# Reordering the last three blocks' steps on TensorE, ScalarE and VectorE in a fused chain of conditioned residual layers

## The reference, cut to what matters

```
x = x + _L0(x, cond)      # low-rank weight decoded from cond, per entry
x = x + _L1(x, cond)      # modulated linear layer, clipped
x = x + _L2(x, cond)      # adapter down, relu, up
# _L3:
h = _ln(_ln(x, pw_g[id], pw_b[id]), cp_g[id4], cp_b[id4])
t = _ln(x, tm_g[id4], tm_b[id4]);  s = _ln(x, ms_g[mask], ms_b[mask])
cat = concat(w0*h, w1*t, w2*(x+mem), w3*(x+noi), w4*(x+res), w5*s)
x = x + _ln(silu(cat @ W1 + b1) @ W2 + b2, int_g, int_be)
```

## Time and profile before

| | us |
|---|---|
| median of 3 executions | 549.65 |
| lowest, highest | 542.51, 550.52 |
| the profiled execution | 539.84 |
| its span | 538.0 |
| TensorE busy in the span | 495.4 (92%) |
| VectorE busy | 407.3 (76%) |
| GpSimd busy | 390.0 (72%) |
| ScalarE busy | 326.5 (61%) |

### The profile page before, as it was taken

One profiled execution on the slowest core, in us unless ns is written; L12 is line 12 of the kernel. 1 busy time (PEld: TensorE's weight loads), 2 busy tenths in 40 slices (PEclk: granted clock), 3 DMA queues, 4 the chain that ended last, 5 costly groups with the idle time before them and its releaser, 6 DMA issues.

```text
span 538.0 us, 9870 instructions
## 1 busy us (share of the span) xinstructions
PE 495.4 (92%) x3408; PEld 354.2 (66%) x3408; DVE 407.3 (76%) x707; ACT 326.5 (61%) x622; POOL 390.0 (72%) x365
## 2 busy tenths in 40 slices
PE   2967968999999999999999999999999999996893
PEld 2944644767677676767676767676767777675682
DVE  1848876768788787878797978787878878885663
ACT  4583647446666575667576667575757665557522
POOL 7468797789777878696968787778777784874221
PEclk9987977899999999999999999999999999998998
DMA  8897714625352252516170707061625241131102
GB/s 300 237 300 190 193 45 95 154 65 122 97 122 78 73 167 60 179 35 204 25 213 0 232 6 208 31 188 51 169 72 154 87 92 40 36 102 57 39 2 78
DMA packets 35621, 61.83 MB, mean 115 GB/s; under 512 B 5985, under 2 KB 18045, under 8 KB 35212
## 3 DMA queue, kind: packets, MB, share of 16 engines
q1 hardware_dynamic: 29532, 44.16, 29.4%
q0 software_dynamic: 5344, 16.87, 10.6%
q10 hardware_dynamic: 720, 0.48, 0.3%
HBM read 52.63 MB, written 8.87 MB: 114 GB/s over the span
## 4 chain that ended last, share of the span: by engine, by line
PE 76%; DVE 10%; ACT 4%; issue 4%; POOL 3%; DMA 1%; DVEq 0%; POOLq 0%; ACTq 0%
PE ps_c L898 12%; PE ps_c L900 11%; PE ps_c L899 11%; PE ps_d L944 9%; PE ps_a L974 6%; PE ps_d L958 6%; PE ps_a L992 3%; PE ps_b L931 3%; PE ps_b L992 3%; PE ps_a L986 3%; DVE tm_t_l L1426 2%; DMA set_wdec<-in_W_dec 1%; PE ps_b L915 1%; PE ps_b L898 1%; PE ps_c L529 1%
## 5 line engine op out<-in xcount | busy, mean ns | idle before, releaser
L1491 POOL DMA_INDIRECT pw_rows<-in_pw,gidx x64 | 63.0, 984 | 17.9 <-issue 17.1
L944 PE MATMUL ps_d<-xm_t,l_w 128*128 128x512 f32 x128 | 59.2, 605 | 0.3 <-DVE h L1417 0.3
L1200 ACT ACTIVATE h<-h,nb_h,rstd_h 128x256 f32<-128x256 f32 x64 | 33.2, 590 | 33.8 <-POOL nb_h L1515 33.7
L1500 POOL TENSOR_TENSOR xm_t<-x_t,style 128x1024 f32<-128x1024 f32 x16 | 30.5, 1905 | 27.9 <-DVE x_t L1330 27.9
L1530 POOL TENSOR_TENSOR h<-xhat,pw_rows 128x1024 f32<-128x1024 f32 x16 | 38.0, 2372 | 11.2 <-ACT xhat L1200 10.7
L944 PEld LDWEIGHTS ps_d<-xm_t,l_w 128*128 128x128 f32 x128 | 23.5, 192 | 25.0 <-issue 23.1
L1549 POOL TENSOR_TENSOR w_up<-up_rep,ugub 128x1024 f32<-128x1024 f32 x16 | 37.9, 2367 | 2.2 <-issue 2.0
L958 PE MATMUL ps_d<-x_t,down_w 128*64 128x256 f32 x256 | 34.1, 413 | 5.8 <-DVE x_t L1352 5.8
L1535 POOL TENSOR_TENSOR h<-h,pw_rows 128x1024 f32<-128x1024 f32 x16 | 38.2, 2390 | 1.3
L1551 POOL TENSOR_TENSOR w_up<-w_up,ugub 128x1024 f32<-128x1024 f32 x16 | 38.2, 2387 | 1.3
L898 PE MATMUL ps_b<-w_h,act_t_l 128*128 128x256 f32 x128 | 38.4, 300 | 0.4 <-DVE act_t_l L1439 0.4
(11 more groups left out here) (239 smaller groups left out, 1537.2 us busy)
## 6 DMA issues: line engine op xcount, KB each, us to landing
ugub<-ugub_scratch SPq DMA_DIRECT2D x32, 512.0 KB, 6.5
x_t<-in_x_t SPq DMA_DIRECT2D x16, 512.0 KB
out<-y_out SPq DMA_DIRECT2D x15, 512.0 KB, 8.1
set_wdec<-in_W_dec SPq DMA_DIRECT2D x2, 1920.0 KB, 9.5
set_wdec<-in_int_W SPq DMA_DIRECT2D x1, 1536.0 KB, 9.9
set_wdec<-in_nets_rows SPq DMA_DIRECT2D x1, 1152.0 KB, 12.5
pw_rows<-in_pw,gidx POOLq DMA_INDIRECT x64
set_wdec<-in_nets_W SPq DMA_DIRECT2D x1, 768.0 KB, 5.0
```

Of the source, the lines that this page charges most:

```text
L944: m = eng.matmul(ps_l1[:, o, :], l1_w[:, k, o * P:(o + 1) * P], xm_t[:, k, :], start=k == 0, stop=k == KB - 1)
L1200: m = eng.activation(out[:, j, :], src[:, j, :], ACT.Identity, bias=nb[k][:, j:j + 1], scale=rstd[k][:, j:j + 1])
L1491: eng.indirect_dma_start(pw_rows[c.ring][:, j, :], None, t["pw"], bass.IndirectOffsetOnAxis(ap=gidx[c.ring][:, j:j + 1], axis=0)).then_inc ...
```

## The change

Three `end` lists are put into another order; no step is added or taken out, and the lists of GpSimd and of the DMA queue (SyncE) are the same.

```
 TensorE
-  (pe_w1_tm, 14), (pe_xht, 15), (pe_cp, 15), (pe_w1_h, 14), (pe_tm, 15), (pe_shift, 15),
+  (pe_w1_tm, 14), (pe_w1_h, 14), (pe_xht, 15), (pe_cp, 15), (pe_tm, 15), (pe_shift, 15),
 ScalarE
-  (act_hnorm, 14), (act_sil0, 13), (act_hh, 14), (act_sil1, 13), (act_x3, 15),
-  (act_msh, 14), (act_xnorm, 15), (act_tmh, 14), (act_onehot, 15), (act_ysquare, 13),
-  (act_x3h, 15), (act_xht, 15), (act_sil0, 14), (act_hnorm, 15), (act_sil1, 14),
+  (act_hnorm, 14), (act_sil0, 13), (act_sil1, 13), (act_hh, 14), (act_x3, 15),
+  (act_xnorm, 15), (act_msh, 14), (act_tmh, 14), (act_onehot, 15), (act_ysquare, 13),
+  (act_x3h, 15), (act_sil0, 14), (act_sil1, 14), (act_xht, 15), (act_hnorm, 15),
 VectorE
-  (v_tmprod, 15), (v_sil1, 14), (v_hprod, 15), (v_tmlow, 15), (v_msprod, 15),
-  (v_hlow, 15), (v_mslow, 15), (v_ygain, 14), (v_ynorm, 14), (v_sil0, 15),
+  (v_sil1, 14), (v_tmprod, 15), (v_hprod, 15), (v_tmlow, 15), (v_hlow, 15),
+  (v_msprod, 15), (v_mslow, 15), (v_ygain, 14), (v_ynorm, 14), (v_sil0, 15),
```

## The result

| | before | after |
|---|---|---|
| median, us | 547.02 (4 executions) | 536.32 (4 executions) |
| lowest, highest, us | 542.51, 550.52 | 535.06, 536.55 |
| profiled execution, span, us | 539.84, 538.0 | 535.06, 533.2 |

The ratio is 0.9863, 95% interval 0.9831 to 0.9895: 1.4% faster. It compares executions in the faster of the kernel's two states; the two medians by themselves would give 0.980, because two of the four executions of before took about 550 us. The forecast was a saving of 5.7 us, 1.0%, and a median of 543.9.

A forecast was written before the change was run, and what follows sets the result against it. TensorE bounds the kernel, stopping for ScalarE and VectorE steps late in their lists. Losses of 7.6 us less new stops of 0.8 and 1.2 leave 5.6; the walk's 5.7 off 549.65 gives 543.9 us, range 534 to 549.

The forecast's parts named there:

- rival 3: Whole executions: most fall like the lower one, giving median 536.8 or 534.1 us with the same mechanism; chance 0.14.
- Block 13's bank 1: ScalarE's silu pair begins near 481.4 and ends near 482.6, so TensorE's 1.18 us loss goes.
- Block 15's `xhat`: ScalarE's norm runs 486.2 to 488.1, leaving TensorE a stop of 0.8 us where 3.24 were.
- The clock: TensorE's W2 of block 13: 1.43 us lost at 1.2 GHz behind the 3.17 us stop is saved.
- h part ahead of the transposes: TensorE, block 14's h part moved forward: a new 1.2 us stop at block 15's `pe_tm`, waiting for `xh_t`.
- The covers: Block 15 on VectorE: h's product is ready 0.9 us and s's low part 0.8 us before TensorE asks.
- rival 2: Block 15's h product or s's low part comes late, costing about 1 us more: 545.0 us; chance 0.12.
- The sum: W2 of block 14 starts near 511.0 and the end moves 5.7 us earlier: span 532.3, median 543.9.
- The clock row: Profile of the changed kernel: a digit under 9 behind slice 36 would show the prediction wrong.
- the median before: Whole kernel: 549.65 us, 9.8 above the profiled execution, taken as it is as base for the 5.7 us saving.
- Rival 1: TensorE's clock dips behind a remaining stop of 0.8 or 1.2 us; 1.43 us stays, 545.4 us; chance 0.11.
- rival 5: Clock stays low from the 0.8 us stop to block 15's `pe_tm`: 6.0 us slower, 555.7 us; chance 0.03.

The follow-up runs named there:

- Run 6: Kernel before with 20 matmuls of constants put into TensorE's 3.2 us stop ahead of L1006 of block 14; median 539.84 us, ratio 0.9979.
- Run 3: Changed kernel with TensorE's old list: block 15's transposes ahead of block 14's h part again; median 539.11 us, ratio 0.9931 to the kernel before.
- run 5: Changed kernel with VectorE's product of s of block 15 ahead of h's low part again; median 536.97 us, ratio 0.9929 to the kernel before.
- run 2: Changed kernel with ScalarE's list at block 13 put back as before; median 542.75 us, ratio 1.0011 to the kernel before.
- run 4: The whole changed kernel measured again, 12 executions; median 536.75 us, ratio 0.9925 to the kernel before.
- run 1: Kernel before with only ScalarE's list at block 13 reordered: bank 1's silu ahead of h's copy, x's norm ahead of s's copy; median 537.22 us, ratio 0.9897.
- run 7: Changed kernel with block 15's transposes ahead of block 14's h part and xh_t ahead of both silus; median 538.46 us, ratio 0.9889 to the kernel before.

## Why the prediction was right

It was right in direction and mechanism, and in how much the change takes off the tail. The time was not: 536.32 us was measured and 543.9 forecast, a miss of 7.6 us that is larger than the saving itself. What came is rival 3, the spread of executions with the same mechanism, at 536.8 us; it had a chance of 0.14 and is why the range reached down to 534. The mechanism first, step by step, all shifted by the 1.0 us that the traces differ at 484:

- *Block 13's bank 1.* Forecast: silu pair from about 481.4, no wait at L1070. The trace has 482.44 - 1.0 = 481.4, and none.
- *Block 15's `xhat`.* Forecast 486.2, stop 0.8. Measured 487.21 - 1.0 = 486.2, stop 0.74. The copy of s at 489.02, its low part at 490.09 (forecast 489.1 on the old axis): covered as said.
- *The clock.* I took 1.43 us as saved because the 3.17 us stop caused the dip. Run 6, where the stop is filled and the dip is gone, bears that out.
- *h part ahead of the transposes.* Forecast: a new stop of 1.2 us released by `xh_t`. Measured 1.19. Run 3 shows what the move is worth: without it the stop is 2.39.
- *The covers.* h's product of block 15 ends at 505.43 + 1.23 = 506.66 and TensorE asks at 507.62: 0.96 us, forecast 0.9. s's low part ends at 513.21 + 1.23 = 514.44, forecast on this axis 514.4, and TensorE asks at 515.17: 0.73 us, forecast 0.8. Neither broke; rival 2 did not come.
- *The sum.* W2 of block 14 begins at 511.90 - 1.0 = 510.9; forecast 511. Tail shorter by 5.81 us; forecast 5.7. The span, forecast 532.3 from an execution that began as that of before did, came out at 533.2, of which 1.0 lies ahead of the change.
- *The clock row.* A digit under 9 behind slice 36 was to be a sign of being wrong. The row has one, the 7 of slice 40, but the fall lies behind TensorE's last matmul (524.51), so the sign was drawn too widely; that of before has an 8 there too.

The size of the median was off for a reason outside the change. The term that failed is the median before, 549.65 of three executions, which I took as it was. Over 60 further executions of before its medians were 542.41 and 542.05, and none was above 548.25. 542.2 less 5.8 is 536.4. So two of the first three executions were unusually slow, by chance or for a cause that is not known, and the mechanism has no part in that difference.

Two things in the prediction need mending. Rival 1, the dip that stays, was placed against the changed kernel on the ground that 0.45 and 1.17 us had cost no clock; run 5 shows a dip behind a stop of 1.19, with about the same price, 1.5 us. The trace of one execution could not rule it out. That the profile of the first result shows none is in part luck: of four profiles with this stop one has the dip. The Trainium skill, "TensorE: Matmul & The Clock Gate", section "A second HAM failure mode: psum-queue depth-cycling", says that short idles between groups of matmuls can come often enough for the clock to swing between its two rates. The traces bear this out only in part: run 5 has one fall, behind one stop, and no repeated swing, and the two profiles of the changed kernel have none. And the price of the dip behind the 3.17 us stop was taken as one number, 1.43; run 2 shows it at over 2.5. So the whole change may remove more than 5.7 us in some executions and give 1.5 us back in others. How often each happens, and so the average, was not measured: the traces show one execution each, and the sums of whole executions mix it with the start of the kernel.

## What to carry to other kernels

When lists of steps are written out by hand, walk the steps through with durations from the trace: each start is the later of "inputs there" and "engine free". Here that gave tails to within 0.2 us in every experiment in which the clock stayed up. What a walk doesn't give is the clock: every stop of TensorE of 1.19 us or more carries a further 1.4 us or more at risk here, so a step that fills a stop can pay even if it makes nothing else earlier (run 6). And where executions differ by 1%, compare traces from a marked instruction behind the part that varies, not spans.

## What the runs showed of the hardware

The granted clock fell from 1.00 to 0.50 (2.4 to 1.2 GHz) behind stops of 3.17, 3.19, 2.39 and 1.19 us, and not behind stops of 1.17, 1.15 and, in three other profiles (first result, runs 2 and 4), 1.19 us. It fell at the end of the stop at the earliest (run 2) and 1.8 us behind it at the latest (run 5), and stayed down for 3.4 us in three of the four cases (before, where the prediction's rival 5 had read 4, and runs 3 and 5) and for 6.8 in run 2. The price of one fall was 1.4 us at the least and over 2.5 at the most. That the stop is the cause was tested for the one of 3.17 us alone, by filling it (run 6); for the shorter ones it is argued from the order in time. I had expected a stop of one length to have one price.

The start of the kernel takes different times in different executions, though its code is the same: those of run 4 come in groups some 5 us apart (535.7 to 537.3 and 541.3 to 542.3). In the three profiles whose clock row begins with 9987595 or 9987596 (runs 1, 4 and 7) block 14's shift starts at 490.9 to 491.8, in run 2 (9987795) at 488.9, and in the other six (9987977, 9977985, 9987986) at 483.5 to 485.0. Why was not looked into.
